# Experts in tiles of 128 rows, their second weights resident in SBUF, and masks of half the width, in a two-layer transformer kernel

## The reference: what is computed

```
x = x + attn_a(layernorm(x))   # 8 heads of 16, causal, scores + head_scale * geo
x = x + ffn(layernorm(x))      # routed experts
x = x + attn_b(layernorm(x))   # 16 heads of 8, not causal
x = x + ffn(layernorm(x))      # the same experts again
```

```
logits = tgt @ Wr.T + br;  top_v, top_i = top_k(logits, 2);  top_w = softmax(top_v)
h   = relu(tgt @ W1[e].T + b1[e])      # 128 -> 512
o_e = h @ W2[e].T + b2[e]              # 512 -> 128
out = layernorm(tgt + sum_e w_e * o_e) * gamma + beta
```

## Time and profile before

| | us |
|---|---|
| median of 3 runs (lowest, highest) | 1011.74 (1009.86, 1013.29) |
| profiled execution, its own time | 1008.01 |
| its span, first to last instruction | 1006.2 |
| layer 0, attention stage | about 0 to 265 |
| layer 0, expert stage | about 280 to 430 |
| layer 1, attention stage | about 430 to 805 |
| layer 1, expert stage | about 816 to 967 |
| final layer norm | about 967 to 1006 |

### The profile page before, as it was taken

The page is one execution under the profiler, slowest core; times in us unless marked ns, Lnnn a source line. Parts: engine busy times, 40 slices in busy tenths (PEclk is TensorE's granted clock), DMA queues, the critical chain, the costliest instruction groups (busy, mean ns, idle before and its releaser), DMA issues.

```text
span 1006.2 us, 22168 instructions
## 1 busy us (share of the span) xinstructions
PE 813.6 (81%) x6318; PEld 574.9 (57%) x6318; DVE 647.6 (64%) x2334; ACT 481.9 (48%) x1129; POOL 434.8 (43%) x510
## 2 busy tenths in 40 slices
PE   2799999986189999915998999899998359999930
PEld 1355555554179999902554555555554149999920
DVE  3346767665346666645788778887884526666657
ACT  2456666654023333312676566657775213333323
POOL 4002444435735555521335444545232515666643
PEclk9999999999589999955899799989997669999975
DMA  6545554431277888616343444334320167777754
GB/s 181 126 95 118 128 127 126 126 83 44 76 218 229 229 231 234 183 42 169 109 120 93 118 122 120 90 103 124 104 76 23 42 190 228 232 232 230 228 158 129
DMA packets 111618, 141.89 MB, mean 141 GB/s; under 512 B 14896, under 2 KB 90544, under 8 KB 108976
## 3 DMA queue, kind: packets, MB, share of 16 engines
q1 hardware_dynamic: 102208, 121.10, 44.0%
q0 software_dynamic: 9088, 18.89, 5.7%
q10 hardware_dynamic: 256, 1.08, 0.4%
HBM read 102.88 MB, written 36.66 MB: 139 GB/s over the span
## 4 chain that ended last, share of the span: by engine, by line
PE 56%; DVE 16%; issue 11%; DMA 7%; ACT 4%; POOL 3%; SPq 3%; DVEq 0%; POOLq 0%; ACTq 0%
PE attn L1307 14%; PE score L1298 7%; PE max L1298 7%; DVE mx L905 5%; PE max L660 5%; PE attn L693 5%; PE score L636 3%; PE misc L729 3%; PE misc L701 2%; POOL xs L1165 2%; DMA qst<-scr 2%; PE attn L1289 2%; PE misc L759 2%; PE max L608 2%; PE score L608 1%
## 5 line engine op out<-in xcount | busy, mean ns | idle before, releaser
L905 DVE TENSOR_REDUCE mx<-max 128x2 f32<-128x512 f32 x352 | 238.3, 683 | 97.4 <-PE max L660 94.2
L430 ACT ACTIVATE prob<-score 128x512 f32<-128x512 f32 x352 | 204.9, 602 | 125.1 <-PE score L636 122.0
L1390 POOL DMA_INDIRECT ys<-yt,idw x156 | 150.2, 963 | 149.1 <-DVE yt L1361 123.7
L339 POOL TENSOR_TENSOR rstd<-rstd,halfm 128x2 f32<-128x2 f32 (+1 forms) x65 | 51.3, 789 | 312.5 <-DVE rstd L332 312.3
L660 PE MATMUL max<-kst,qst 72*128 72x256 bf16 (+2 forms) x768 | 144.4, 279 | 24.3 <-DVE mx L905 16.8
L1307 PE MATMUL attn<-wsl,prob 128*128 128x128 f32 x1248 | 152.1, 275 | 0.0
L1165 POOL DMA_INDIRECT xs<-row,index x128 | 126.5, 989 | 47.3 <-issue 28.6
L1307 PEld LDWEIGHTS attn<-wsl,prob 128*128 128x128 f32 x1248 | 145.7, 192 | 0.1
L636 PE MATMUL score<-qst,kst 74*128 74x256 bf16 (+2 forms) x768 | 141.3, 274 | 3.0 <-DMA qst<-mparts 2.7
L1326 ACT ACTIVATE prob<-score,wsl 128x256 f32<-128x256 f32 x78 | 37.0, 474 | 218.7 <-PE score L1298 218.7
L693 PE MATMUL attn<-prob,vaug 128*32 128x256 f32 (+1 forms) x1536 | 119.5, 384 | 1.3 <-ACT prob L430 0.6
(11 more groups left out here) (142 smaller groups left out, 1235.9 us busy)
## 6 DMA issues: line engine op xcount, KB each, us to landing
wsl<-in_wall SPq DMA_DIRECT2D x78, 578.0 KB, 4.2
scr<-parts SPq DMA_DIRECT2D x32, 384.0 KB, 2.9
qst<-scr SPq DMA_DIRECT2D x64, 192.0 KB
xt<-xs SPq DMA_DIRECT2D x78, 132.0 KB
kst<-scr SPq DMA_DIRECT2D x16, 576.0 KB
row<-row SPq DMA_DIRECT2D x32, 128.0 KB, 3.5
yg<-ys SPq DMA_DIRECT2D x32, 128.0 KB, 2.8
kst<-scr SPq DMA_DIRECT2D x16, 192.0 KB
```

The lines of the kernel that those rows point to most:

```text
L339: nc.gpsimd.tensor_tensor(rstd[:, which, slot, :, 1], rstd[:, which, slot, :, 0], half, ALU.pow)\
L430: nc.scalar.activation(prob[:, g % 2, k, :], pS[(g * NB + k) % 2][:, :], ACT.Exp)\
L905: nc.vector.tensor_reduce(mx[:, sl[4], a:a + 2 * n - 1:2], pM[(g * NB + k) % 2][:, :].rearrange("p (h w) -> p h w", h=n), axis=AX.X, op=AL ...
L1390: nc.gpsimd.indirect_dma_start(out=ys, out_offset=bass.IndirectOffsetOnAxis(ap=idw[:, k, c, 0:1].bitcast(U32), axis=0), in_=yt[:, k, c, :] ...
```

## The change

The tile of the expert stage becomes 128 rows, which makes `NJ` = (8192 + 8 x 127) // 128 = 71 tiles in a layer. The second product's weights and both biases of all 8 experts are loaded once at the start of the kernel into `wres` (2.64 MB), by a DMA from ACT's queue. For each tile SP loads only the first product's weights (`w1s`, 262 KB) and 128 rows, four tiles ahead. Since a tile's expert is known only at run time, PE, ACT and DVE now read the expert numbers too: every 8 tiles (`GROUP`) each of them loads 8 numbers into registers, checks each against its bounds, and computes from them the address of each operand in `wres`. SP loads 8 row numbers and 8 expert numbers in the same way. The hardware loop is gone: the 71 tiles stand one after another in the program. ACT does the ReLU of chunks 0, 2 and 3, DVE that of chunk 1. The wide masks are written only over the halves that hold the diagonal mask, with 256 columns in place of 512.

```diff
-TILE = 256
+TILE = P
-SLOTS = 3
+SLOTS = 4
+GROUP = 8
...
-        past = sb("past", [P, NJ, E])
-        skipped = sb("skipped", [P, NJ, E])
+        past = yg[:, :, :, :, :].rearrange("p r k c d -> p (r k c d)")[:, 0:NJ * E].rearrange("p (j e) -> p j e", e=E)
...
-        wsl = sb("wsl", [P, SLOTS, WCOLS])
+        wres = sb("wres", [P, E, WCOLS - F])
+        w1s = sb("w1s", [P, SLOTS, F])
...
                     if c == "wide":
-                        mask(dst[:, :], maske_w[:, :, :, :].rearrange("p a b q -> p (a b q)"))
+                        mask(dst[:, :].rearrange("p (a w) -> p a w", a=2)[:, :, 0:P], maske_n[:, 0:2, :])
...
-                        mask(dst[:, :], maskm_w[:, :, :, :].rearrange("p a b q -> p (a b q)"))
+                        mask(dst[:, :].rearrange("p (a w) -> p a w", a=2)[:, :, P:T], maskm_n[:, 0:2, :])
...
+        def loads_of(ops, table, at):
+            _, values = nc.values_load_multi_w_load_instructions(
+                table[0:1, at:min(at + GROUP, NJ)], engines=[ops.engine], min_val=0,
+                max_val=E - 1 if table is t_exp_i else E * REGION + (SPARE - 1) * TILE)
+            return values
...
 def sp_experts
+            for j in range(NJ):
+                k = j % SLOTS
+                if j % GROUP == 0:
+                    rows = loads_of(nc.sync, t_row_i, j)
+                    chosen = loads_of(nc.sync, t_exp_i, j)
+                sp.wait_ge("idw_done", NJ * li + j + 1 - SLOTS)
+                sp.wait_ge("xT_ps", NJ * li + j + 1 - SLOTS)
+                sp.wait_ge("xf_done", NJ * li + j + 1 - SLOTS)
+                nc.sync.dma_start(xt[:, k, :], xs[bass.ds(rows[j % GROUP], TILE), :]).then_inc(s_(f"xt_in{k}"), 16)
+                sp.wait_ge("h_ps", (NJ * li + j + 1 - SLOTS) * FC)
+                nc.sync.dma_start(w1s[:, k, :], wall[bass.ds(chosen[j % GROUP], 1), :, 0:F]
+                                  .rearrange("a p c -> p (a c)")).then_inc(s_(f"w_in{k}"), 16)
...
 def pe_experts
+            for j in range(NJ):
+                if j % GROUP == 0:
+                    chosen = loads_of(nc.tensor, t_exp_i, j)
+                w = wres[:, bass.ds(chosen[j % GROUP], 1), :].rearrange("p a c -> p (a c)")
...
+                for n, f in enumerate((0, 1, 2, 3)):
+                    if f == 1:
+                        pe.wait_ge("h_dve", n0 + j + 1)
+                    else:
+                        pe.wait_ge("h_act", (n0 + j) * 3 + (1, 0, 2, 3)[f])
+                    mm = nc.tensor.matmul(pY[:, 0:P], hT[:, f, :], w[:, f * P:(f + 1) * P],
+                                          start=(f == 0), stop=(f == FC - 1), skip_group_check=True)
...
 def dve_experts
+            for j in range(NJ):
+                if j:
+                    results(j - 1)
+                e = expert(j)
+                dve.wait_ge("h_ps", (n0 + j) * FC + 2)
+                dve.wait_ge("y_ps", n0 + j)
+                b1 = wres[:, e, FC * P + 1].rearrange("p a -> p a")
+                nc.vector.tensor_scalar(hT[:, 1, :], pH[1][:, 0:TILE], b1, 0.0, ALU.add, ALU.max)\
+                    .then_inc(s_("h_dve"), 1)
+                if j + 1 < NJ:
+                    columns(j + 1)
...
         def _(act):
+            nc.scalar.dma_start(wres[:, :, :], wall[:, :, F:WCOLS].rearrange("e p c -> p e c")).then_inc(s_("experts_in"), 16)
```

More of the change, by code:

```diff
@@ L278, in build @@
         for name in "y_in scr_w st_in m_in t_cp scat w_in xt_in y_out".split():
-            for i in range(RING):
+            for i in range(max(RING, SLOTS)):
                 s_(f"{name}{i}")
@@ L1201, in dve_tiles @@
             if li:
-                for k in range(SLOTS):
-                    dve.wait_ge(f"w_in{k}", 16 * (NJ // SLOTS))
+                dve.wait_ge("c_x", B)
+                dve.wait_ge("xT_ps", NJ)
             nc.vector.tensor_copy(pad_row[:, :], run[:, :])
@@ L1226, in dve_tiles, with turn @@
             link(dve, nc.vector.tensor_copy(run[:, :], first_row))
-        def tile_loop(eng, body):
-            first = SLOTS + 1
-            turns = (NJ - first - 1) // SLOTS
-            for j in range(first):
-                body(j, j % SLOTS)
-            with eng.engine.Fori(0, turns) as i:
-                for k in range(first, first + SLOTS):
-                    body(At(i, SLOTS, k), k % SLOTS)
-            for j in range(first + turns * SLOTS, NJ):
-                body(j, j % SLOTS)
-        def turn(li, j, k):
-            return (j - k) // SLOTS + 1 + NJ // SLOTS * li
-        def before(j, n):
-            return isinstance(j, int) and j < n
+        def turn(li, j):
+            k = j % SLOTS
+            return j // SLOTS + 1 + len(range(k, NJ, SLOTS)) * li
+        def loads_of(ops, table, at):
[3 more added lines that the diff above has]
+            return values
         def pad(ops, experts):
@@ L1303, in body @@
                 pe.wait_ge("ysum_sb", n0 + j)
-                for f in range(FC):
-                    pe.wait_ge("h_dve" if f % 2 else "h_act", (n0 + j) * 2 + f // 2 + 1)
-                    for c in range(QC):
-                        mm = nc.tensor.matmul(pY[:, c * P:(c + 1) * P], hT[:, f, c * P:(c + 1) * P],
-                                              wsl[:, k, F + f * P:F + (f + 1) * P],
-                                              start=(f == 0 and c == 0), stop=(f == FC - 1), skip_group_check=True)
+                for n, f in enumerate((0, 1, 2, 3)):
[5 more added lines that the diff above has]
+                                          start=(f == 0), stop=(f == FC - 1), skip_group_check=True)
@@ L1349, in results, with expert @@
[L1349 to L1352 removed]
+            chosen = {}
+            dve.wait_ge("experts_in", 16)
+            dve.wait_ge("tiles_known", li + 1)
+            def expert(j):
+                if j % GROUP == 0:
+                    for n, e in enumerate(loads_of(nc.vector, t_exp_i, j)):
+                        chosen[j + n] = e
+                return bass.ds(chosen[j], 1)
@@ L1376, in dve_experts @@
-            columns(0, 0)
-            tile_loop(dve, body)
-            results(NJ - 1, (NJ - 1) % SLOTS)
+                dve.wait_ge("ysum_sb", n0 + j + 1)
+                nc.vector.scalar_tensor_tensor(out=yt[:, k, :], in0=ysum[:, k, :], scalar=idw[:, k, 1:2],
+                                               in1=xf[:, k, :], op0=ALU.mult, op1=ALU.add).then_inc(s_("yt_sb"), 1)
+            columns(0)
+            for j in range(NJ):
+                if j:
[6 more added lines that the diff above has]
+                    .then_inc(s_("h_dve"), 1)
+                if j + 1 < NJ:
+                    columns(j + 1)
```

154 lines of the change are left out of this document (55 added, 99 removed).

## The result

The changed kernel takes 1126.3 us in the median of 4 runs (1125.5 to 1127.1), the kernel before 1010.8 beside it: a ratio of 1.115, with a 95% interval from 1.111 to 1.119. It is 115 us slower. I had forecast 1070, with a range up to 1108, so the sign was right and the size was not.

What follows compares the result with a forecast made beforehand. PE was taken to bound the expert stages. Tiles +36.8, reads +28.8, stage starts +5.0, ends -3.1, masks -10, kernel start +1.5 made +59 us on 1008.0: 1067, on the runs' median 1070; range 1015 to 1108.

Steps and rivals of the forecast that it cites:

- the groups of reads: Expert stages: once in 8 tiles PE, DVE and ACT read and check 8 numbers; 16 groups of 1.8 us, 28.8 us more.
- The clock, which I had as a rival at 0.13: Rival (1098 us): after each of 16 groups PE runs about one tile at 1.2 GHz, +27 us; chance 0.13.
- the starts of the stages: Start of an expert stage: SP's reads come before the weights, longer tables, smaller loads; +2.5 us a layer, 5.0 more.
- the masks: Attention 0: wide masks of half the width occupy PE for less time; 10 us less, between 4 and 13.7.
- the tiles: Expert stages: 142 tiles of 2.31 us, 328 us, in place of 78 of 3.73, 291 us; 36.8 us more.
- The terms of the loop: Expert tile: last matmul, `ysum`, `yt`, DVE's ReLU of chunk 1, second product from chunk 1 on; sum 2.31 us.
- PE's own floor of 1.89: Expert tile of 128 rows: 8 x 0.111 + 0.11 + 8 x 0.111 = 1.89 us if PE stayed the bound.
- The rival with that floor (982 us): Expert stages: waits overlap and loads are hidden, so PE stays the bound at 1.89 us a tile; -29.4 us, chance 0.15.
- The kernel start: Start of the kernel: the resident weights, 2.64 MB, load beside the first loads; 1.5 us more.
- the end of the kernel: End of an expert stage: one scatter less follows the last tile, smaller `yt`; 1.5 us in a layer, 3.1 less.
- The checks beside the queue (1042): Rival: the checks run beside the engine's queue, so the 28.8 us are gone and the loop stays; chance 0.13.

## Why the forecast was too low

- **The step that failed is the groups of reads.** I had put 16 x 1.8 = 28.8 us, and "SP's groups later on are hidden: it is 2.5 tiles ahead, 5.8 us, and loses 4.3 in 18". The 140 intervals between tiles sum to 399.9 us, 87.7 more than 140 x 2.23; 70.9 of them are the checks. Three things are in it. PE's own block takes 2.9 us where I had 2.13, and makes a hole of 2.5 rather than 1.8. SP's block is 5.2 us rather than 4.3, because the read of 8 numbers takes 0.53 and not the 0.29 of one, and it is not wholly hidden; that the lead has to hold the 3.73 us of the landing too would explain it. And the two don't overlap: PE reads only once it has waited for SP's rows.
- **The clock, which I had as a rival at 0.13**, came as well. It is 25.7 us of PE's busy time. The rival's 27 is close to it partly by luck: its own numbers, 16 tiles of 3.8 in place of 2.3 us, make 24. The earlier trace rows had shown a clock of 0.76 behind a hole; here two holes, of together 2.6 to 4.9 us, stand where I had argued with one of 1.8. The rival and the failed step are one mechanism: I should have priced a hole with the slow tiles behind it.
- **The other terms nearly cancel.** Against the forecast of 59 us for the span and 117.5 measured, the groups are 59 over, the starts of the stages 5 and the masks 8; the tiles are 11 under. The rest are terms of 4 us and less.
- **The tile was right: 2.23 us, forecast 2.31.** The terms of the loop can be read at 363 us of the changed kernel's trace:

```profile
360.01 0.35 DVE L1369 TENSOR_SCALAR prob<-score,wres 128x128 f32<-128x128 f32 x1 [0.23 <-PE max L1292]
...
360.50 0.93 PE L1303 MATMUL attn<-wres,prob 128*128 x6 [0.15 <-DVE prob L1369]
...
363.50 0.61 PE L1292 MATMUL score<-prob,w1s 128*128 128x128 f32 x4
363.81 0.29 DVE L1353 TENSOR_TENSOR ysum<-attn,wres 128x128 f32<-128x128 f32 x1 [0.95 <-PE attn L1303]
...
364.21 0.35 DVE L1358 SCALAR_TENSOR_TENSOR yt<-ysum,idw,xf 128x128 f32<-128x128 f32 x1
...
364.48 0.35 DVE L1369 TENSOR_SCALAR prob<-score,wres 128x128 f32<-128x128 f32 x1
```

  From the last matmul's start, 0.11 ahead of 363.50, to `ysum` 0.42 (I had 0.31 + 0.12), `ysum` 0.29, a gap of 0.11, `yt` to ReLU 0.27, ReLU 0.35, all as forecast within 0.04. From the ReLU's end to chunk 1 are 0.14 (360.36 to 360.50) and not 0.27. From there to the last matmul are 0.66 for my 0.56, because the second matmul of chunk 1 follows the first by 0.21 and the others by 0.11. I had counted this 0.1, the weight load that can't run ahead of the wait, ahead of the first matmul; the two together are 0.80 against 0.83. The sum is 2.24.
- **PE's own floor of 1.89 was right.** With PE one tile ahead the shortest tiles take 1.89 to 1.92 us. The rival with that floor (982 us) failed by the argument that the prediction held against it: even without a price for the computations the loop through DVE is longer, 2.04 measured, 2.07 forecast. So no overlap of waits in this order of work could reach the floor, only another order.
- **Start of an expert stage: +5.1 in layer 0, forecast 2.5.** From DVE's last `x` of attention 0 to the first product are 31.8 us against 26.7, and 25.9 in the variant without checks; layer 1 has 31.6, 26.4 and 25.8. SP's checks make most of it: without them the distance is 27.9, without those of the other engines 30.2. What the forecast had at nothing is the 2.0 us between 27.9 and 25.9. "The first group of a layer lies beside SP's start" is where it failed: PE starts its block after the first transpose, so after SP's.
- **Masks: about 3, forecast 10.** From the first to the last `x` of attention 0 are 176.7 us against 178.6, and masks alone gave 3, which is not clear of noise. In 150 us of it PE's busy time fell by 4.8, from 134.98 to 130.21, and its granted clock from 0.99 to 0.96. That the work taken away ended mostly in waits for others fits these rows, but no run took it apart. The kernel start cost 0.9 at the first `x`, forecast 1.5; the end of the kernel gave 2.4 beside the shorter last tile (42.0 us from the last first product to the end, against 45.9), forecast 1.5 in a layer.
- **The checks beside the queue (1042)** did not occur: a block of 2.9 us makes a hole of 2.50. The Trainium skill, Advanced Engine Details and Errata, section Sequencer Loop, says that an engine's instructions can be queued while its sequencer executes one of its own. No run here contradicts it. Here it helps little: only the last matmuls of the second product had been handed out when the block began, and the 0.4 us between block and hole are all that runs beside it.

## What to carry to other kernels

Before an engine is made to read run-time values, sum its sequencer's whole block (read, checks, address) and ask which blocks come one after the other; add the slow clock that the hole brings on PE. A lead is worth its time less the landing of what it fetches. Halving a tile halves neither the waits nor the fixed latencies, and can leave even the bound engine without gain: test it with constant addresses first, since that gives the most that the change can bring in that order of work. An engine that the profile shows as busy can still be waiting: compare the distance between its instructions with that of a stretch where nothing is waited for.

## What the runs showed of the hardware

- Reading 8 numbers into registers took 0.52 us on SP, 0.55 on ACT, 0.59 on PE and 0.60 on DVE; reading one took 0.27 on SP. Each check took 0.147 + 0.018 us on SP, ACT and PE, 0.183 + 0.023 on DVE; from one to the next were 0.25 us on SP, 0.22 on ACT and 0.28 on PE and DVE.
- A register address for an operand cost mostly 46 ns a computation on PE and ACT and 65 to 69 on DVE, and 0.20 us in a tile of 2.23.
- Matmuls of 128 columns in f32 started 0.112 us apart, also where each second one had a wait of its own that was already met. Behind a wait that was not met, the second one followed the first by 0.21.
- The DMA engines gave 338 GB/s at a 99% share.
- Behind the holes of a group in the changed kernel (2.6 to 4.9 us together) the next tile took 3.1 to 3.8 us in place of 2.23, the one after it 2.2 to 2.9; in the stretch shown the granted clock was 0.54. Without SP's checks the holes were 2.5 to 2.8 us, and the next tile took 2.3 to 3.6.
